# Diagonal part of a graph layer: PE products against transposes with a GpSimd product, with a new order on every engine

## The reference

```python
x = _layernorm(x + _L0_gnn_ref(x, L0_gnn_a, adj, adj))     # pair scores, softmax over i, sigmoid
x = _layernorm(x + _L1_gnn_ref(x, adj, ...))               # masked attention, then a two-matrix MLP
x = _layernorm(x + _L2_gnn_ref(x, adj, W, e, bias))
x = _layernorm(x + _L3_gnn_ref(x, adj, W, a_src, a_dst))   # masked attention, elu
```

```python
out = einsum('ij,bjg->big', A * M, h0) + einsum('ij,bjg->big', A * (1.0 - M), h1)   # M = eye(512)
# h0 = x @ W[0], h1 = x @ W[1]
```

## Time and profile before

| | |
|---|---|
| median of 3 runs | 1213.48 us (1211.66 to 1216.96) |
| the profiled execution | 1216.8 us, of which the span of the profile is 1214.8 us |
| granted PE clock, mean of the span | 0.966 |
| PE, PEld, DVE, ACT, POOL busy | 91%, 75%, 89%, 84%, 35% of the span |
| DMA | 35.95 MB, 30 GB/s on the mean |

### The profile page before, as it was taken

One profiled execution on the slowest core, in us unless ns is written; L12 is line 12 of the kernel. 1 busy time (PEld: TensorE's weight loads), 2 busy tenths in 40 slices (PEclk: granted clock), 3 DMA queues, 4 the chain that ended last, 5 costly groups with the idle time before them and its releaser, 6 DMA issues. The chain is left out here.

```text
span 1214.8 us, 29110 instructions
## 1 busy us (share of the span) xinstructions
PE 1110.8 (91%) x7721; PEld 913.0 (75%) x7752; DVE 1083.8 (89%) x4214; ACT 1016.1 (84%) x2581; POOL 431.0 (35%) x800
## 2 busy tenths in 40 slices
PE   4788899999999999999999999999999999999863
PEld 3456688777777888777877888777877888778753
DVE  6887899999999999999999999999999999997543
ACT  3456789999999999999899999999999999998654
POOL 3022343333434433333434433333434433333311
PEclk8599999999999999999999999999999999999986
DMA  2000001000111001001111011001111011000000
GB/s 74 27 18 27 27 28 36 24 28 26 35 35 35 31 30 35 19 26 33 35 35 35 26 35 35 17 26 35 35 35 35 26 35 35 18 27 28 18 9 18
DMA packets 59459, 35.95 MB, mean 30 GB/s; under 512 B 3872, under 2 KB 54816, under 8 KB 59424
## 3 DMA queue, kind: packets, MB, share of 16 engines
q1 hardware_dynamic: 59424, 35.54, 9.5%
HBM read 18.75 MB, written 8.39 MB: 22 GB/s over the span
## 5 line engine op out<-in xcount | busy, mean ns | idle before, releaser
L434 POOL TENSOR_TENSOR lnve_Z<-lnmv_Z,consts 128x4 f32<-128x4 f32 x32 | 39.1, 1222 | 302.9 <-DVE lnmv_Z L1098 302.9
L752 PE MATMUL ps<-hE,pTE 128*128 128x128 f32 x1024 | 132.8, 278 | 0.0
L680 PE MATMUL ps<-xsA,pA 128*128 128x128 f32 x1024 | 124.7, 281 | 8.3 <-ACT xsA L1557 8.3
L680 PEld LDWEIGHTS ps<-xsA,pA 128*128 128x128 f32 x1024 | 118.9, 195 | 13.7 <-ACT xsA L1557 13.7
L752 PE MATMUL ps<-hB,pTB 128*128 128x128 f32 x1024 | 125.1, 275 | 0.0
L752 PEld LDWEIGHTS ps<-hE,pTE 128*128 128x128 f32 x1024 | 122.5, 193 | 1.6
L812 PE MATMUL ps<-att_j,xD 128*128 128x512 f32 x256 | 123.3, 605 | 0.0
L769 PE MATMUL ps<-gin_j,hgat 128*128 128x512 f32 x256 | 121.6, 599 | 0.0
L752 PEld LDWEIGHTS ps<-hB,pTB 128*128 128x128 f32 x1024 | 119.5, 192 | 0.1
L1118 DVE SCALAR_TENSOR_TENSOR wE<-ps,hE,y2E 128x512 f32<-128x512 f32 x128 | 92.0, 745 | 24.5 <-ACT y2E L1579 18.7
L1547 ACT ACTIVATE pA<-vA,nmA,rirA 128x512 f32<-128x512 f32 x128 | 104.8, 819 | 3.0 <-DVE vA L1247 3.0
(11 more groups left out here) (237 smaller groups left out, 3031.2 us busy)
## 6 DMA issues: line engine op xcount, KB each, us to landing
xA<-in_x_dram SPq DMA_DIRECT2D x32, 256.0 KB, 2.8
xrA<-in_x_dram SPq DMA_DIRECT2D x32, 256.0 KB, 3.0
xrB<-xB SPq DMA_DIRECT2D x32, 256.0 KB, 2.2
out_dram<-xout SPq DMA_DIRECT2D x32, 256.0 KB, 2.2
adj_i<-in_adj_dram SPq DMA_DIRECT2D x1, 1024.0 KB, 8.0
a<-in_L_gnn_a_dram SPq DMA_DIRECT2D x2, 64.0 KB, 4.6
w_sb<-in_L_gnn_W_dram SPq DMA_DIRECT2D x2, 64.0 KB, 5.6
l2w<-in_L_gnn_W_dram SPq DMA_DIRECT2D x2, 64.0 KB, 4.9
```

Source lines behind the costliest of these rows:

```text
L680: last = mm(at("aggA")[:, i * P:(i + 1) * P], pA[:, j, i * P:(i + 1) * P], xsA[:, j], start=(j == 0), stop=(j == NT - 1))
L752: last = mm(at("agg" + n)[:, i * P:(i + 1) * P], att[n]["pT"][:, i, j], att[n]["h"][:, j, 0:P], start=(j == 0), stop=(j == NT - 1))
```

## The change

- PE's `scale_xD` becomes `transpose_xD`, four plain transposes. ACT's `copy_xTD` now fills a new buffer `xTD`, and POOL multiplies it elementwise (128 x 512, float32, both inputs in SBUF) by `diag2`, the diagonal spread over all partitions, into `xTdD`. `diag2` is made once in turn 4, and `dia` now shares its memory with `xout`.
- Six small DVE operations are written in another form (`tensor_scalar` and `tensor_copy` become `tensor_tensor` or `scalar_tensor_tensor`) with the same values.
- Every `turn(t)` and `IN_BANK` have a new order.

```diff
+            def diag_D(g):
+                if g.first:
+                    pool.wait_ge(*after("diag_ready", 1))
+                pool.wait_ge(s["xTD_ready"], g.now)
+                pool.wait_ge(s["outD_ready"], g.last)
+                pool.tensor_tensor(xTdD[:], xTD[:], diag2[:], ALU.mult).then_inc(s["xTdD_ready"], 1)
...
-            def scale_xD(g):
...
-                for i in range(NT):
-                    last = mm(at("xTD")[:, i * P:(i + 1) * P], xD[:, i], dia[:, i], start=True, stop=True)
-                last.then_inc(s["xD_scaled"], 1)
+            def transpose_xD(g):
                 pe.wait_ge(s["applied_C"], g.now)
                 bank_free(g, "xTD")
+                transpose("xTD", xD).then_inc(s["xD_transposed"], 1)
...
-                v.tensor_scalar(cenA[:, :, 1], cenA[:, :, 1], irA, None, ALU.add).then_inc(s["tirA"], 1)
+                v.tensor_tensor(cenA[:, :, 1], cenA[:, :, 1], irA.to_broadcast([P, NT]), ALU.add).then_inc(s["tirA"], 1)
...
-                v.tensor_copy(sp_parts[0], cenA[:]).then_inc(s["hiA"], 1)
+                v.tensor_tensor(sp_parts[0], cenA[:], one, ALU.mult).then_inc(s["hiA"], 1)
...
             def copy_xTD(g):
-                act.wait_ge(s["xD_scaled"], g.now)
-                act.wait_ge(s["outD_ready"], g.last)
-                a.copy(xTdD[:], at("xTD")).then_inc(s["xTdD_ready"], 1)
+                act.wait_ge(s["xD_transposed"], g.now)
+                act.wait_ge(s["xTdD_ready"], g.last)
+                a.copy(xTD[:], at("xTD")).then_inc(s["xTD_ready"], 1)
```

More of the change, by code:

```diff
@@ L158, in resnorm_gnn @@
         xTB = sb("xTB", [P, N])
+        xTD = sb("xTD", [P, N])
         xTE = sb("xTE", [P, N])
@@ L250, in resnorm_gnn @@
         ge_i = xTE[:].bitcast(BF16).rearrange("p (t e) -> p t e", t=NT)
-        dia = sb("dia", [P, NT, P])
+        dia = xout
         loops = xE
@@ L631, in _, with diagonal @@
             edge_values0, edge_values1, edge_values2, edge_values3 = (edge_values(i) for i in range(NT))
+            def diagonal(once):
+                pe.wait_ge(*after("dia_ready", NT))
+                bank_free(once, "diag")
+                for i in range(NT):
+                    last = mm(at("diag")[:, i * P:(i + 1) * P], ones[:], dia[:, i], start=True, stop=True)
+                last.then_inc(*signal("diag_in_psum"))
             def transpose_att(j):
@@ L1211, in middle_A @@
                 dve.wait_ge(s["rest1A"], g.now)
-                v.tensor_copy(sp_parts[1], r1A[:]).then_inc(s["midA"], 1)
+                v.tensor_tensor(sp_parts[1], r1A[:], one, ALU.mult).then_inc(s["midA"], 1)
             def rest_A1(g):
@@ L1219, in low_A @@
                 dve.wait_ge(s["rest2A"], g.now)
-                v.tensor_copy(sp_parts[2], r2A[:]).then_inc(s["spA"], 1)
+                v.tensor_tensor(sp_parts[2], r2A[:], one, ALU.mult).then_inc(s["spA"], 1)
             def v_A(j):
@@ L1362, in turn @@
+                t.run(middle_A, 0)
+                t.once(past_table0, 1)
+                t.run(rest_A1, 0)
+                t.once(bias_row1, 1)
+                t.once(row_minimum2, 2)
+                t.run(low_A, 0)
+                t.run(L_E0, 4)
+                t.once(split_low, 1)
+                t.run(L_E1, 4)
                 t.once(match_edges0, 1)
-                t.run(shift_A, 0)
-                t.once(split_rest0, 1)
+                t.run(M_E0, 4)
+                t.run(M_E1, 4)
@@ L1379, in turn @@
-                t.once(normal_rows1, 2)
-                t.run(L_E1, 4)
-                t.once(bias_row1, 1)
-                t.run(M_E0, 4)
-                t.once(normal_rows2, 2)
-                t.run(M_E1, 4)
-                t.once(split_low, 1)
-                t.once(past_table1, 1)
-                t.run(L_E2, 4)
-                t.once(mask_adj, 0)
-                t.run(L_E3, 4)
-                t.once(row_minimum3, 2)
-                t.run(M_E2, 4)
-                t.run(v_A0, 0)
@@ L1393, in turn @@
-                t.once(bias_row2, 1)
-                t.run(v_A1, 0)
+                t.once(past_table1, 1)
+                t.once(bias_row2, 1)
+                t.run(L_E2, 4)
+                t.once(row_minimum3, 2)
+                t.run(L_E3, 4)
+                t.once(normal_rows1, 2)
+                t.once(mask_adj, 0)
+                t.run(v_A0, 0)
+                t.once(normal_rows2, 2)
+                t.run(v_A1, 0)
+                t.run(M_E2, 4)
+                t.once(past_table2, 1)
@@ new lines, in turn @@
+                t.run(y_C, 2)
+                t.run(recip_A, 0)
+                t.once(select_rows0, 0)
+                t.run(mult_B3, 1)
+                t.once(self_loops, 1)
+                t.run(bn_C, 2)
+                t.once(outside1, 1)
+                t.once(weigh_x, 0)
+                t.run(y1_E, 4)
+                t.once(select_rows1, 0)
+                t.run(join_C, 2)
+                t.run(y_E, 4)
+                t.run(bn_B, 1)
+                t.once(row_minimum0, 1)
+                t.run(bn_E, 4)
@@ L1484, in _, with copy_diag @@
             exp_rows0, exp_rows1, exp_rows2, exp_rows3 = (exp_rows(i) for i in range(NT))
+            def copy_diag(once):
+                act.wait_ge(*after("diag_in_psum", 1))
+                a.copy(diag2[:], at("diag")).then_inc(*signal("diag_ready"))
             def copy_att(j):
```

270 lines of the change are left out of this document (129 added, 141 removed), and 22 rows, old and new, of the table IN_BANK.

## The result

The changed kernel takes 1221.83 us (median, 1219.94 to 1223.57) against 1215.18 us (1211.66 to 1218.77) of the kernel before: ratio 1.0054, 95% interval 1.0039 to 1.0069. The forecast was 1224 us and a turn of 34.6 to 34.9 us. As a difference it was +11 us over a median of 1213.5; measured are +6.65 over 1215.18.

The account below looks back on a forecast made before the run. A ring over DVE, POOL and ACT, with DVE on it nearly everywhere, was taken to set the 34.24 us turn. Per turn -0.1 + 0.6 = +0.5, times 26 = +13, fill and drain -2: 1213.5 + 11, rounded 1224 us; range 1203 to 1237.

Parts of the forecast that it names:

- The ring: The 34.24 us turn: first part from `lnmv_Z` over POOL and ACT to `y1E`, 13.10; second part DVE alone, 21.14.
- PE's 0.46 us: Time PE gets back each turn from transposes in place of matmuls; claimed to shorten no turn, only lengthen PE's waits.
- The product: POOL's multiply of 512 elements: 1233 ns, from 628.25 to 629.5 us, started by ACT's copy, holding DVE through SBUF access.
- DVE up to `M_E0`: DVE's stretch from `y1E` to the first `wE<-wE,no_i`, 12.50 us before; its terms summed to -0.10 us.
- `t2B` lies over the wait for `rirA`: -0.45: On DVE ahead of `cenA`: `t2B` fills the wait for POOL's `rirA`, -0.45 us, less if POOL is late.
- the five other terms: DVE up to `M_E0`: `lnmv_C` +0.30, `veA` -0.10, last `spA` +0.13, `spA` to `r1A` +0.12, small forms -0.10.
- The hold of `M_E0`: POOL's product holds DVE's `M_E0` until 629.5 us: +0.6 us a turn, bounds 0 and 1.23.
- The small forms: Six small DVE operations at 0.16 us in place of 0.17 to 0.23: -0.10 us a turn.
- Fill and drain: Time before the loop's first turn and behind its last store: -2 us, a choice, bounds -10 and +8.
- miss `M_E0`: Rival: the copy of `xTD` ends later, the product runs behind `M_E0` without stall; 1207 us, chance 0.20.
- PE's returned time: Rival: PE, the fullest engine, sets the pace, so 0.46 us a turn come back; 1199 us, chance 0.10.
- Heavier hits: Rival: the product comes a little later, to 629.95, stall 1.1 us, turn +1.0; 1237 us, chance 0.13.

Follow-up runs that it names:

- a_pe_scale: Changed kernel with PE's matmuls by the diagonal as before and without POOL's product; 1215.21 us, 1.0004 of the kernel before.
- a_var_m_z_pe: Changed kernel with `veA` ahead of `t1B`, `L_E2` ahead of `M_E0`, `lrelu_A3` behind `L_B1`, diagonal on PE, no product; 1198.66 us.
- a_var_first: Changed kernel with `veA` put ahead of `t1B` on DVE; 1218.71 us, 1.0037 of the kernel before.
- b_product: Kernel before, in its own orders, with the transposes, copy and POOL's product in place of the diagonal matmuls; 1242.60 us, 1.0221.
- a_offset_later: Changed kernel with `t2B` put back behind `cenA`; 1222.64 us, 1.0063 of the kernel before.
- b_forms: Kernel before with only the six small DVE operations in their two-input form; 1210.03 us, 0.9955.
- a_m_later: Changed kernel with `L_E2` put ahead of `M_E0` and `M_E1` on DVE; 1218.45 us, 1.0035 of the kernel before.

## Why the prediction was right, point by point

*The ring.* Its second part, DVE alone, carries the whole change, as forecast. The first part took 651.01 - 637.93 = 13.08 us against 13.10. One detail was wrong without cost: `y1E` was to wait longer and shows no wait, since a 0.39 us wait for PE now lies ahead of a `pTB` in the same stretch. `y1E` still starts 0.11 us after the end of ACT's `euE` (616.18 and 616.07; before 650.73 and 650.63), so ACT and DVE arrive together. The second part is not DVE's work alone either: a gap of 0.31 us ahead of `lnve_B` (620.36), which the prediction's reading left out, stood in it before, and one of 0.29 ahead of `prA` after.

*PE's 0.46 us* shortened nothing that shows: a_pe_scale and a_var_m_z_pe, which give them up together with the product, are not slower.

*The product.* Its duration was 1.27 us for the 1233 ns worked out. Its place has to be counted from `y1E`, which starts at 616.49 before and 616.18 after. ACT's copy ended 11.65 us behind `y1E`, for 11.7 forecast, and the product ran from 11.96 to 13.23 for 11.8 to 13.0. It came 0.2 us late because POOL was busy to 628.16: the late `rirA` set the start, not ACT. In a_var_first, where POOL waits for ACT's copy, it is 11.82. "Whoever comes second stands still until the first is through" is shown for the product: where it holds something, the held instruction ends 0.54 or 0.55 us (`M_E0`, five kernels) or 0.05 to 0.06 us (`spA`, two kernels) after it. The section of the Trainium skill named in the prediction (SBUF — State Buffer, Who interferes with whom) also lists casts among what can contend, and a DVE instruction with at most one SBUF input, outside the modes that use both ports, as what doesn't; the cast of b_product (1.14 us) and the `wE` from PSUM (0.7 us each beside the product) agree. The order of issue, which the prediction quotes from there, does not fit one row: `rirA` begins at 625.06, 0.04 us ahead of `t2B`, and yet is the one that is lengthened.

*DVE up to `M_E0`: the term that was mis-sized.* "`t2B` lies over the wait for `rirA`: -0.45" did not come. `t2B` covered 0.66 us and lengthened POOL's power from 0.69 to 1.25, so 0.59 us of wait stayed; a_offset_later shows it, with 0.69 and a wait of 0.60. The prediction had kept this back as "should POOL be late, up to 0.45 of it comes back". It knew that `t2B` had lengthened a power of `rstd_A` before, and did not ask the same of `rirA`. The sum became +0.40 in place of -0.10: the wait had been put at -0.45 and came out at 0.59 - 0.45 = +0.14; the five other terms had been put at +0.35 together and came out at (12.90 - 0.59) - (12.50 - 0.45) = +0.26. What each of the five came to was not taken apart.

*The hold of `M_E0`* was +0.20 for +0.6. That is the same error seen from behind: the product ends at a nearly fixed point, and DVE arrived late by its wait. In a_var_first `M_E0` starts 12.36 us behind `y1E`, close to the forecast's 12.4, and the hold is 0.59, nearly the 0.6 forecast. So the sum of a turn, +0.58 for +0.5, came out right because two errors of nearly equal size, +0.50 and -0.40, stand against each other. They are tied to each other by the product's end, so this is not all luck; but four of the signs that the prediction gave for being right did not come: no wait ahead of `cenA`, a longer one ahead of `y1E`, `M_E0` longer by 0.6 us, and the product starting 0.65 us ahead of it (0.94).

*The small forms* gave 0.10 a turn in b_forms, the number of the -0.10. Since the wait ahead of `cenA` is 0.15 us shorter there than in the earlier trace rows, the mechanism (shorter instructions) is not shown by it. Beside the product they help nothing (35.18 against 35.14).

*Fill and drain* were -8.6 us (-10.2 and +1.6) for -2. It is within the bounds -10 to +8 and is the reason for 1222 instead of some 1228. 3.8 us are due to SP's and POOL's lists. Without the product the first store is 5.1 us earlier still (a_pe_scale, 203.00), at a mean granted clock of 0.86 from 36 to 60 us where the changed kernel had 0.68 and the kernel before 0.57; what of the fill is the clock's and what its cause is was not taken apart. The remaining 6.4 us are the net of the product's 5.1 us the other way, of 0.3 us that the forms gave in b_forms, and of some 11 us that are left for the orders of DVE, ACT and PE, by subtraction alone; they stay open.

*The rivals.* The product did not miss `M_E0`; a_m_later makes it so and gains 0.17 us, but no more, since `cenA`'s wait was not in that rival's account. PE's returned time did not set the pace. Heavier hits exist in before's orders (b_product, +0.90). In the chances, the parts of "within 0.5%" add up to 0.21, not 0.23, and "slower" by the same parts is 0.53, not 0.51.

## What to carry over

In these runs a DVE instruction that reads two tiles from SBUF, or casts from it, waits out a POOL product that runs: put instructions with a PSUM input beside it, and look at the small ones between them too, since 8 elements can cost 1.1 us. Before filling a wait for POOL, ask whether the filler holds POOL: a two-input one of 0.66 us lengthened the awaited power by 0.56 us. And take away two stalls in a row together. Removed alone, the first handed most of its time to the second (the wait of 0.59 went, the hold grew from 0.20 to 0.59, the turn fell by 0.11); the second alone gave its own 0.17; together they gave 0.72.

## What the runs showed beyond that

POOL's write-only operations tell the two forms apart. In turn 0 before, `cenA` as TENSOR_SCALAR stood beside a MEMSET of 1.81 us and took 1.90 us:

```profile
13.66 1.81 POOL L405 MEMSET pE<- 128x2048 bf16 x1
...
13.60 1.90 DVE L1197 TENSOR_SCALAR cenA<-cenA,rirA 128x4 f32<-128x4 f32 x1 [0.61 <-POOL rirA L452]
```

In b_forms, where the form is all that differs, the same `cenA`, again starting 0.06 us ahead of the MEMSET, took 0.16 us:

```profile
13.74 1.81 POOL L405 MEMSET pE<- 128x2048 bf16 x1
...
13.68 0.16 DVE L1201 TENSOR_TENSOR cenA<-cenA,rirA 128x4 f32<-128x4 f32 x1 [0.61 <-POOL rirA L452]
```

And in the changed kernel `spA` (0.19) and `r1A` (0.17) lie wholly within the MEMSET:

```profile
14.08 1.82 POOL L408 MEMSET pE<- 128x2048 bf16 x1
...
14.28 0.19 DVE L1224 TENSOR_TENSOR spA<-cenA,ones 128x8 bf16<-128x8 f32 x1
14.50 0.17 DVE L1228 TENSOR_TENSOR r1A<-cenA,spA 128x8 f32<-128x8 f32 x1
```

And POOL's power `lnr_E` does not hold DVE, though DVE can lengthen a power (`rirA` above): `y_A`, two inputs in SBUF, took its usual 0.69 us at 622.21, in the midst of `lnr_E`, which ran from 622.08 to 623.14:

```profile
622.08 1.06 POOL L443 TENSOR_TENSOR lnr_E<-lnve_E,consts 128x4 f32<-128x4 f32 x1
...
622.21 0.69 DVE L1283 SCALAR_TENSOR_TENSOR y_A<-thA,xrA 128x512 f32<-128x512 f32 x1
```
